# Causal attention in a two-layer block: the causal mask of the transposed scores moves from TensorE to a GpSimd select on the probabilities, and PV of two key tiles stand together

## The chip, the cores and the metric

One core of one Trainium2 chip. The metric is the device time of one execution in microseconds; the time of before is the median of its runs, 2668.89 us.

## The reference

Two layers on x of shape (2, 2048, 256), each with a layer norm, an attention s, a mixture of experts passed through silu, g, and x + s * g. The change touches the attention of the first layer alone. It is exact causal softmax attention of 16 heads of 16 columns:

```python
scores = jnp.einsum('bhcd,bhsd->bhcs', qi, k) * scale
mask = kpos[None, :] <= qpos[:, None]
scores = jnp.where(mask, scores, jnp.finfo(scores.dtype).min)
p = jax.nn.softmax(scores, axis=-1)
return (None, jnp.einsum('bhcs,bhsd->bhcd', p, v))
```

## The kernel before, in words

The program runs stage after stage: projections of the first layer, its attention (`stage_attention`), its experts, a join, and the second layer in windows. An engine's instructions run in the order in which its function lists them.

`stage_attention` works in 8 groups: 4 groups of 4 heads (GH) for each of the 2 sequences. A group has 4 chunks of 512 queries (QC, CH). Each chunk c looks at 4 (c + 1) key tiles of 128 keys, 40 in a group and 320 in all. The last 4 tiles of a chunk hold the diagonal; there only the queries from `lo` on are used, so that the widths are 512, 384, 256 and 128. Every attention has two passes:

- The maxima pass ("A"). Scores with queries on the partitions go to one of three PSUM banks, `ring` (L721, and L724 adds the mask `mask_qk` on the diagonal block). VectorE takes the maximum (L859, `take`). After each chunk VectorE splits the negated maxima into three bf16 parts (`split`, L866 to L870), TensorE turns them (L731), VectorE copies them out (L876), and SyncE's queue puts them into three more rows of `qa` (L691).
- The probabilities pass. "S" is the score with keys on the partitions (L774) for one head: the three more rows subtract the row's maximum. Two heads share a buffer `pss`, of which there are two. On a diagonal tile L777 adds `mask_kq`, -1e30 above the diagonal, by a second matmul against the identity on the first 128 columns. ScalarE takes the exponential of two heads in one instruction (L836) into `probs`, which keeps two key tiles: four slots of two heads. "PV" (L792) multiplies the probabilities with v, four heads side by side, each with 32 columns of the array, and gathers in `acc`; a column of ones in `vg` gathers the sum. It is fp32; each product has two records in the profile. At the end of a chunk ScalarE copies `acc` to `sums` ("COPY", L844); TensorE transposes that through the ring ("O", L802), VectorE divides (L906, L909), and ScalarE's queue stores it.

The order is written out by `attention_steps`. `weave` goes over the 40 pairs (chunk, key tile): it lists 4 S, puts as many steps of the maxima pass between them as their share of the columns asks for, and then lists the PV of the pair before. So PV of tile n - 1 stands behind the scores of tile n. The maxima run half a group ahead (LEAD): the second half of a group's own maxima, then the first half of the next group's; the last group has only its own second half. O and the turn of the maxima come 6 scores late. GpSimd has no part in this: in this stage it sets constants, clears the table of the experts and issues 32 scatters (L668). 

TensorE's waits: a score of the first head of two waits until the exponential that used the same `pss` is done; a maxima matmul waits until VectorE has taken the bank three steps back; PV waits for the second exponential of its tile. ScalarE's exponential waits for its scores and for the PV that used the same slots of `probs`.

Of the kernel before, what the change touches and what calls it, by code (L numbers as in the profile page):

```python
# [16 lines left out]
BF16 = mybir.dt.bfloat16  # L17
# [3 lines left out]
ALU = mybir.AluOpType  # L21
ACT = mybir.ActivationFunctionType
X = mybir.AxisListType.X

P = 128
B, S, D = 2, 2048, 256
T = B * S
NT = T // P
CH = 512
TC = CH // P  # L30
# [5 lines left out]
NEG = -1e30  # L36
# [7 lines left out]
GH = 4  # L44
HG = H // GH
KT = S // P
QC = S // CH
QR = 6 * HD
MR = QR + 3
# [56 lines left out]
def build_constants(nc, keep):  # L106

    with ExitStack() as ctx:
        st = Stage(nc, ctx, "c_")
# [4 lines left out]
        def _(pool):  # L114
            ch = Chain(pool, pool_step)
            ch.link(pool.memset(keep["identity"][:, :], 0.0))
            ch.link(pool.affine_select(out=keep["identity"][:, :], in_=keep["identity"][:, :], compare_op=ALU.not_equal,
                                       fill=1.0, base=0, pattern=[[-1, P]], channel_multiplier=1))
# [8 lines left out]
                                       fill=NEG, base=0, pattern=[[-1, P]], channel_multiplier=1))  # L127
            ch.link(pool.affine_select(out=keep["mask_kq"][:, :], in_=keep["zero16"][:, :], compare_op=ALU.is_ge,
                                       fill=NEG, base=0, pattern=[[1, P]], channel_multiplier=-1))

# [362 lines left out]
def attention_steps():  # L493
# [39 lines left out]
    def weave(ahead):  # L533
# [15 lines left out]
        for n, (c, j) in enumerate(pairs):  # L549
            for h in range(GH):  # L550
                steps.append(("S", c, j, h))
                done += width(c, j)
                advance()
                for item in late:
                    item[1] -= 1
                while late and late[0][1] <= 0:
                    steps.append(late.pop(0)[0])
            if n:
                pc, pj = pairs[n - 1]
                steps.append(("PV", pc, pj))  # L560
                if pj == TC * (pc + 1) - 1:
                    steps.append(("COPY", pc))
                    late.append([("O", pc), 6])
        c, j = pairs[-1]
        steps += ahead + [u for u, _ in late] + [("PV", c, j), ("COPY", c), ("O", c)]
        return steps
# [10 lines left out]


def stage_attention(nc, io, keep, dram):

# [4 lines left out]
    n_s = sum(u[0] == "S" for u in steps) // 2  # L585
    n_pv = sum(u[0] == "PV" for u in steps)
    parts_q, parts_k = (0, 0, 1, 1, 0, 2), (0, 1, 0, 1, 2, 0)
    n_loads = len(parts_q) * QC + len(parts_k)
    with ExitStack() as ctx:
# [3 lines left out]
        vg = [st.sb(f"vg{u}", [P, KT, GH, 32]) for u in range(2)]  # L593
        probs = st.sb("probs", [P, 4, 2, CH])
        best = st.sb("best", [P, QC, GH * TC, QC])
        neg = st.sb("neg", [P, GH * TC])
        neg_rest = st.sb("neg_rest", [P, GH * TC])
        neg_parts = st.sb("neg_parts", [P, P // (GH * TC), GH * TC], BF16)
        neg_rows = st.sb("neg_rows", [3 * GH * TC, 2, P], BF16)
        sums = st.sb("sums", [P, CH])  # L600
        inv = st.sb("inv", [P, TC, GH])
# [13 lines left out]
        m_landed = [st.sem(f"m_landed{c}") for c in range(QC)]  # L615
        o_stored = [st.sem(f"o_stored{c}") for c in range(2)]
        dve_step = st.sem("dve_step")
        cleared, scattered = st.sem("cleared"), st.sem("scattered")
# [33 lines left out]
        def _(pool):  # L652
# [14 lines left out]
            for t in range(NT):  # L667
                pool.indirect_dma_start(dram["expert_in"], bass.IndirectOffsetOnAxis(ap=keep["slot_put"][:, t:t + 1], axis=0),  # L668
                                        keep["xn_all"][:, t, :], None, bounds_check=E * CAP0 - 1, oob_is_err=False
                                        ).then_inc(scattered, 16)  # L670
            pool.wait_ge(scattered, 16 * NT)

# [41 lines left out]
        def _(pe):  # L714
# [34 lines left out]
            for g, i, u, order in groups(pe):  # L749
                idx = pv = m = r = 0  # L750
                next_seen = False
                for s in order:
# [11 lines left out]
                    elif s[0] == "S":  # L764
# [6 lines left out]
                        if e == 0:  # L771

                            pe.wait_ge(exp_done, primed + g * n_s + max(idx - 1, 0))
                        ins = pe.matmul(pss[idx % 2][:, e, lo:CH], kb[u][0:MR, h, j * P:(j + 1) * P],  # L774
                                        qa[u][0:MR, c, h, lo:CH], start=True, stop=(j < TC * c))
                        if j >= TC * c:
                            ins = pe.matmul(pss[idx % 2][:, e, lo:lo + P], keep["identity16"][:, :],  # L777
                                            keep["mask_kq"][:, :], start=False, stop=True)
                        if e == 1:
                            ins.then_inc(s_ready, 1)  # L780
                            idx += 1
                    elif s[0] == "PV":
                        _, c, j = s
                        lo = max(0, j - TC * c) * P
                        pe.wait_ge(exp_done, primed + g * n_s + 2 * pv + 2)
                        if c == 0 and j == 0:
# [4 lines left out]
                        for h in range(GH):  # L791
                            ins = pe.matmul(acc[32 * h:32 * h + 32, lo:CH], vg[u][:, j, h, :],  # L792
                                            probs[:, 2 * (pv % 2) + h // 2, h % 2, lo:CH],
                                            start=(j == 0), stop=(j == TC * (c + 1) - 1))
# [13 lines left out]
        def _(act):  # L808
# [11 lines left out]
            for g, i, u, order in groups(act):  # L820
                idx = r = pv = r_turn = 0
                turned_at = None
                for s in order:
# [6 lines left out]
                    if s[0] == "S" and s[3] % 2 == 1:  # L830
# [3 lines left out]

                        act.wait_ge(pv_done, primed + g * n_pv + max(idx // 2 - 1, 0))
                        act.activation(probs[:, idx % 4, :, lo:CH], pss[idx % 2][:, :, lo:CH], ACT.Exp).then_inc(exp_done, 1)  # L836
                        idx += 1
# [1075 lines left out]
def make_program(nc, io, out, upto=7):  # L1913
# [9 lines left out]
    with ExitStack() as ctx:  # L1923
# [7 lines left out]
            "mask_qk": st.sb("mask_qk", [P, P], BF16),  # L1931
            "mask_kq": st.sb("mask_kq", [P, P], BF16),
            "expert": st.sb("expert", [P, E, NT]),
# [70 lines left out]
```

## Time and profile before

| | us |
|---|---|
| median of 3 runs | 2668.89 |
| lowest of them | 2668.31 |
| span of the profiled execution | 2692.8 |
| the first attention's busy stretch in it, 214 to 1157 us | 943.0 |

The profiled execution has no time of its own beside its span; the span is 23.9 us (0.9%) above the median of the timed runs. In the timeline a row gives start, duration, engine, line, operation, output and inputs, how many like it were merged, and in brackets the idle time before it and what ended it. PE is TensorE, PEld its weight load, DVE VectorE, ACT ScalarE, POOL GpSimd.

### The profile page before, as it was taken

The page shows a single profiled execution, that of the slowest core. Times are in us where ns is not written, and L with a number is a line of the kernel's source. Part 1 is how long each engine was busy: PE and PEld are TensorE (multiplying, and loading weights), DVE is VectorE, ACT ScalarE, POOL GpSimd, SP SyncE. Part 2 cuts the span into 40 slices and gives each one's busy share as a digit, 9 for nine tenths or more (in the row PEclk, how much of TensorE's full clock was granted, in tenths as well). Part 3 has the DMA queues.
Part 4 walks back from the last instruction along what each step waited for, and adds up shares of the span by engine and source line. Part 5 has one row for each costly group of instructions (what it writes and reads, how often), then busy time and mean ns, then how long its engine had stood idle before and what let it go on. Part 6 is the DMA issues. An engine that isn't in the chain of part 4 may idle for free. (4 is left out here: it accounts for less than half of the span.)

```text
span 2692.8 us, 51134 instructions
## 1 busy us (share of the span) xinstructions
PE 2451.3 (91%) x16420; PEld 1589.0 (59%) x16420; DVE 1846.2 (69%) x3682; ACT 1406.8 (52%) x2776; POOL 815.1 (30%) x647
## 2 busy tenths in 40 slices
PE   5648999999999999969977599999999999999999
PEld 4512333333333333358866477777777777777777
DVE  7757877877787777424438476777667767766776
ACT  3404655656565566755634255555555555555554
POOL 1070000000000000014425355554455555444553
PEclk9858999999999999989988699999999999999999
DMA  4574041321404040033257000000000000000000
GB/s 135 191 170 65 5 62 26 41 52 16 61 6 62 6 60 5 7 127 133 102 177 241 18 13 12 11 13 13 13 13 13 9 11 13 13 13 13 13 9 9
DMA packets 189865, 132.85 MB, mean 49 GB/s; under 512 B 99857, under 2 KB 177687, under 8 KB 189712
## 3 DMA queue, kind: packets, MB, share of 16 engines
q1 hardware_dynamic: 160048, 100.06, 15.4%
q10 hardware_dynamic: 24160, 14.16, 2.2%
q0 software_dynamic: 5504, 16.69, 1.7%
q8 instruction: 83, 1.36, 0.2%
q14 instruction: 70, 0.57, 0.1%
HBM read 84.43 MB, written 46.14 MB: 48 GB/s over the span
## 5 line engine op out<-in xcount | busy, mean ns | idle before, releaser
L859 DVE TENSOR_REDUCE a_best<-a_ring 128x1 f32<-128x512 f32 (+3 forms) x1280 | 700.9, 604 | 214.0 <-PE a_ring L721 123.0
L836 ACT ACTIVATE a_probs<-a_pss 128x1024 f32<-128x1024 f32 (+3 forms) x640 | 554.0, 895 | 452.6 <-PE a_pss L777 228.7
L721 PE MATMUL a_ring<-a_kb,a_qa 96*128 96x512 bf16 (+3 forms) x1280 | 453.0, 365 | 67.2 <-DVE a_best L859 32.3
L774 PE MATMUL a_pss<-a_qa,a_kb 99*128 99x512 bf16 (+3 forms) x1280 | 433.9, 353 | 15.6 <-issue 7.2
L1771 ACT ACTIVATE w_probs<-w_pss,w_top 128x256 f32<-128x256 f32 x512 | 239.0, 476 | 379.7 <-DVE w_top L1859 365.0
L1606 POOL TENSOR_TENSOR w_probs<-w_probs,w_inv 128x512 f32<-128x512 f32 x256 | 301.0, 1176 | 395.7 <-DVE w_inv L1865 386.3
L962 POOL TENSOR_TENSOR e_w_r<-e_w,e_w_r 128x1024 fp32r<-128x1024 f32 x28 | 67.0, 2402 | 1032.7 <-ACT e_w_r L1035 1032.7
L1629 PE MATMUL w_psw<-wqkv,w_xr 128*128 128x512 f32 x1152 | 301.5, 398 | 11.6 <-POOL w_xr L1563 11.6
L774 PEld LDWEIGHTS a_pss<-a_qa,a_kb 99*128 99x128 bf16 x1280 | 123.5, 98 | 302.6 <-ACT a_probs L836 224.5
L792 PE MATMUL a_acc<-a_probs,a_vg 128*32 128x512 f32 (+3 forms) x2560 | 299.9, 541 | 0.1
L1669 PE MATMUL w_pss<-w_kd,w_qt 128*128 128x256 f32 x1536 | 278.4, 310 | 0.0
L1859 DVE TENSOR_REDUCE w_top<-w_pss 128x2 f32<-128x512 f32 x256 | 176.8, 691 | 141.5 <-PE w_pss L1669 140.7
L721 PEld LDWEIGHTS a_ring<-a_kb,a_qa 96*128 96x128 bf16 x1280 | 126.4, 99 | 223.9 <-DVE a_best L859 128.6
L1629 PEld LDWEIGHTS w_psw<-wqkv,w_xr 128*128 128x128 f32 x1152 | 205.6, 190 | 47.6 <-POOL w_xr L1563 12.1
L1669 PEld LDWEIGHTS w_pss<-w_kd,w_qt 128*128 128x128 f32 x1536 | 222.0, 195 | 4.1
L1629 PE MATMUL w_psw<-we,w_xr 128*128 128x512 f32 x768 | 204.2, 401 | 0.0
L1710 PE MATMUL w_pso<-w_pt,w_v 128*64 128x128 f32 x2048 | 168.3, 285 | 0.1
L1689 PE MATMUL w_pst<-identity,w_probs 128*128 128x128 f32 x1024 | 155.7, 275 | 0.0
L1629 PEld LDWEIGHTS w_psw<-we,w_xr 128*128 128x128 f32 x768 | 134.9, 188 | 22.9 <-issue 0.2
L1689 PEld LDWEIGHTS w_pst<-identity,w_probs 128*128 128x128 f32 x1024 | 123.6, 140 | 31.2 <-issue 5.7
L1882 DVE SCALAR_TENSOR_TENSOR w_y<-w_psw,coef,w_y 128x256 f32<-128x256 f32 x224 | 108.3, 484 | 42.4 <-PE w_psw L1629 23.2
L1710 PEld LDWEIGHTS w_pso<-w_pt,w_v 128*64 128x64 f32 x2048 | 106.5, 136 | 49.6 <-issue 49.1
(223 smaller groups left out, 3771.2 us busy)
## 6 DMA issues: line engine op xcount, KB each, us to landing
e_w<-in_w SPq DMA_DIRECT2D x16, 1024.0 KB, 7.9
qk_parts<-p_parts SPq DMA_DIRECT2D x32, 384.0 KB, 3.7
a_qa<-qk_parts SPq DMA_DIRECT2D x192, 64.0 KB, 2.5
a_kb<-qk_parts SPq DMA_DIRECT2D x42, 256.0 KB, 9.5
p_xin<-in_x SPq DMA_DIRECT2D x8, 512.0 KB, 5.4
v_rows<-p_vout SPq DMA_DIRECT2D x8, 512.0 KB, 5.1
a_vg<-v_rows SPq DMA_DIRECT2D x32, 128.0 KB, 9.1
expert_in<-zero POOLq DMA_DIRECT2D x16, 256.0 KB, 8.3
```

Source lines behind the costliest of these rows:

```text
L721: ins = pe.matmul(bank[:, 0:keys], qa[u][0:QR, i // TC, h, (i % TC) * P:(i % TC + 1) * P], kb[u][0:QR, h, k * CH:k * CH + keys], start=Tru ...
L774: ins = pe.matmul(pss[idx % 2][:, e, lo:CH], kb[u][0:MR, h, j * P:(j + 1) * P], qa[u][0:MR, c, h, lo:CH], start=True, stop=(j < TC * c))
L792: ins = pe.matmul(acc[32 * h:32 * h + 32, lo:CH], vg[u][:, j, h, :], probs[:, 2 * (pv % 2) + h // 2, h % 2, lo:CH], start=(j == 0), stop=( ...
L836: act.activation(probs[:, idx % 4, :, lo:CH], pss[idx % 2][:, :, lo:CH], ACT.Exp).then_inc(exp_done, 1)
L859: vec.tensor_reduce(best[:, i // TC, h * TC + i % TC, k:k + 1], bank[:, 0:keys], X, ALU.max).then_inc(ring_taken, 1)
L1606: pool.tensor_tensor(probs[:, p % 4, :, :], probs[:, p % 4, :, :], inv[:, :, p:p + 1].to_broadcast([P, 2, 2 * P]), ALU.mult).then_inc(p_re ...
L1629: ins = pe.matmul(psw[bank][:, :], xr[a][:, src, k, :], moving(b, k), start=(m == 0), stop=(m == len(pairs) - 1))
L1669: ins = pe.matmul(scores, qt[a][:, p, :], keys[b][:, p, :, :], start=False, stop=(a, b) == PARTS[-1])
L1689: ins = pe.transpose(pst[r % 2][:, 2 * e + role, :], probs[:, p % 4, e, role * P:(role + 1) * P], keep["identity"][:, :])
L1710: ins = pe.matmul(pso[e * DH:(e + 1) * DH, p % 4, :], v[(u + 1 + role) % 2][:, h * DH:(h + 1) * DH], pt[:, p % 2, 2 * e + role, :], start= ...
L1771: ins = act.activation(probs[:, p % 4, e, :], pss[p % 2][:, e, :], ACT.Exp, bias=top[:, e, p:p + 1], accum_out=rows[:, e, p:p + 1])
L1859: vec.tensor_reduce(top[:, :, p], pss[p % 2][:, :, :], X, ALU.max, negate=True).then_inc(top_ready, 1)
```

## The change

- The mask matmul on the transposed scores (L777) is gone, with its constant `mask_kq`. A score of a diagonal tile is written without a mask.
- After the exponential of a diagonal tile GpSimd sets the probabilities of future keys to zero in place, on 2 heads x 128 columns, by an `affine_select`; ahead of it stands an addition of one element per partition into a scratch tile `spare`. GpSimd does so behind its 32 scatters, for every diagonal exponential of all groups.
- PV of a diagonal tile waits for that (`future_cleared`), PV of another tile for the exponential as before.
- PV is listed for two tiles at a time: behind the scores of every even tile n stand PV of n - 2 and of n - 1; the last two of a group stand at its end.
- `probs` keeps four key tiles (KEPT), so that ScalarE waits for the PV four tiles back instead of two.

```diff
-            if n:
-                pc, pj = pairs[n - 1]
+            for pc, pj in (pairs[n - 2], pairs[n - 1]) if n and n % 2 == 0 else ():
                 steps.append(("PV", pc, pj))
                 if pj == TC * (pc + 1) - 1:
                     steps.append(("COPY", pc))
                     late.append([("O", pc), 6])
-        c, j = pairs[-1]
-        steps += ahead + [u for u, _ in late] + [("PV", c, j), ("COPY", c), ("O", c)]
+        c = pairs[-1][0]
+        steps += ahead + [u for u, _ in late] + [("PV", *p) for p in pairs[-2:]] + [("COPY", c), ("O", c)]
...
+KEPT = 4
...
+    n_diagonal = QC * TC * GH // 2
...
-        probs = st.sb("probs", [P, 4, 2, CH])
+        probs = st.sb("probs", [P, KEPT * GH // 2, 2, CH])
...
+            for g, i, u, order in groups(pool):
+                idx = 0
+                for s in order:
+                    if s[0] == "S" and s[3] % 2 == 1:
+                        _, c, j, h = s
+                        if j >= TC * c:
+                            lo, slot = (j - TC * c) * P, idx % (KEPT * GH // 2)
+                            pool.wait_ge(exp_done, primed + g * n_s + idx + 1)
+                            pool.tensor_tensor(spare[:, slot:slot + 1], keep["zero"][:, 0:1], keep["zero"][:, 0:1], ALU.add)
+                            seen = probs[:, slot, :, lo:lo + P]
+                            pool.affine_select(out=seen, in_=seen, compare_op=ALU.is_ge, fill=0.0, base=0,
+                                               pattern=[[0, 2], [1, P]], channel_multiplier=-1).then_inc(future_cleared, 1)
+                        idx += 1
             pool.wait_ge(scattered, 16 * NT)
...
                         ins = pe.matmul(pss[idx % 2][:, e, lo:CH], kb[u][0:MR, h, j * P:(j + 1) * P],
-                                        qa[u][0:MR, c, h, lo:CH], start=True, stop=(j < TC * c))
-                        if j >= TC * c:
-                            ins = pe.matmul(pss[idx % 2][:, e, lo:lo + P], keep["identity16"][:, :],
-                                            keep["mask_kq"][:, :], start=False, stop=True)
+                                        qa[u][0:MR, c, h, lo:CH], start=True, stop=True)
...
-                        pe.wait_ge(exp_done, primed + g * n_s + 2 * pv + 2)
+                        if j < TC * c:
+                            pe.wait_ge(exp_done, primed + g * n_s + 2 * pv + 2)
+                        else:
+                            pe.wait_ge(future_cleared, g * n_diagonal + GH // 2 * (j + 1))
...
-                                            probs[:, 2 * (pv % 2) + h // 2, h % 2, lo:CH],
+                                            probs[:, GH // 2 * (pv % KEPT) + h // 2, h % 2, lo:CH],
...
-                        act.wait_ge(pv_done, primed + g * n_pv + max(idx // 2 - 1, 0))
-                        act.activation(probs[:, idx % 4, :, lo:CH], pss[idx % 2][:, :, lo:CH], ACT.Exp).then_inc(exp_done, 1)
+                        act.wait_ge(pv_done, primed + g * n_pv + max(idx // 2 - KEPT + 1, 0))
+                        act.activation(probs[:, idx % (KEPT * GH // 2), :, lo:CH], pss[idx % 2][:, :, lo:CH], ACT.Exp).then_inc(exp_done, 1)
```

## Rows read from the trace of the kernel before

**Rows 1.** The head of the page: span, busy time by engine.

```profile
span 2692.8 us, 51134 instructions
...
PE 2451.3 (91%) x16420; PEld 1589.0 (59%) x16420; DVE 1846.2 (69%) x3682; ACT 1406.8 (52%) x2776; POOL 815.1 (30%) x647
```

**Rows 2.** Busy time by engine in windows: us, PE, PEld, DVE, ACT, POOL, clock, DMA.

```profile
214.00:1157.00 943.00, 899.55 (x6196) 339.54 (x6196) 711.99 (x1459) 569.05 (x672) 0.00 (x0) 0.99 0.22 33
```

**Rows 3.** Groups of instructions by line, 214 to 1157 us.

```profile
L859 DVE TENSOR_REDUCE a_best<-a_ring 128x1 f32<-128x512 f32 (+3 forms) x1215 | 667.8, 606 | 173.5 <-PE a_ring L721 119.4 <-PE a_ring L724 47.1 <-remote 4.5
L836 ACT ACTIVATE a_probs<-a_pss 128x1024 f32<-128x1024 f32 (+3 forms) x640 | 554.0, 895 | 452.6 <-PE a_pss L777 228.7 <-PE a_pss L774 207.8 <-DVE a_best L859 10.1
...
L792 PE MATMUL a_acc<-a_probs,a_vg 128*32 128x512 f32 (+3 forms) x2560 | 299.9, 541 | 0.1
...
L777 PE MATMUL a_pss<-mask_kq,identity 128*128 128x128 bf16 x512 | 104.9, 222 | 0.0
```

**Rows 4.** Timeline of TensorE around a first diagonal tile.

```profile
1048.67 0.39 PE L774 MATMUL a_pss<-a_qa,a_kb 99*128 99x512 bf16 x1
1048.89 0.22 PE L777 MATMUL a_pss<-mask_kq,identity 128*128 128x128 bf16 x1
1048.95 0.38 PE L721 MATMUL a_ring<-a_kb,a_qa 96*128 96x512 bf16 x1
...
1050.73 0.22 PE L724 MATMUL a_ring<-mask_qk,identity 128*128 128x128 bf16 x1
1050.88 1.06 PE L792 MATMUL a_acc<-a_probs,a_vg 128*32 128x512 f32 x8
1051.88 0.34 PE L774 MATMUL a_pss<-a_qa,a_kb 99*128 99x384 bf16 x1
```

**Rows 5.** Window over eight key tiles without a diagonal.

```profile
656.46:683.09 26.63, 25.80 (x157) 8.67 (x156) 21.80 (x47) 15.96 (x17) 0.00 (x0) 1.00 0.03 7
```

**Rows 6.** Timeline in the same stretch: VectorE, and TensorE's PV and next maxima matmul.

```profile
665.28 2.35 DVE L859 TENSOR_REDUCE a_best<-a_ring 128x1 f32<-128x512 f32 x4 [0.84 <-PE a_ring L721]
...
666.54 1.06 PE L792 MATMUL a_acc<-a_probs,a_vg 128*32 128x512 f32 x8
...
667.77 0.38 PE L721 MATMUL a_ring<-a_kb,a_qa 96*128 96x512 bf16 x1
...
668.19 2.88 DVE L859 TENSOR_REDUCE a_best<-a_ring 128x1 f32<-128x512 f32 x6 [0.56 <-PE a_ring L721]
...
671.70 1.29 DVE L859 TENSOR_REDUCE a_best<-a_ring 128x1 f32<-128x512 f32 x2 [0.63 <-PE a_ring L721]
```

**Rows 7.** Who waited for whom in the same stretch: in all, times, longest.

```profile
PEld a_ring L721 <- DVE a_best L859: 3.5, 10, 0.5
```

**Rows 8.** Timeline at the end of a group.

```profile
1057.38 1.01 PE L792 MATMUL a_acc<-a_probs,a_vg 128*32 128x256 f32 x16
1057.96 0.16 PEld L792 LDWEIGHTS a_acc<-a_probs,a_vg 128*32 128x32 f32 x8 [0.43 <-ACT a_probs L836]
...
1059.10 0.66 PE L802 MATMUL a_ring<-identity,a_sums 128*128 128x128 f32 x4 [0.70 <-ACT a_sums L844]
```

**Rows 9.** Timeline of the tail, where no maxima are left.

```profile
1133.42 3.91 ACT L836 ACTIVATE a_probs<-a_pss 128x1024 f32<-128x1024 f32 x4 [0.27 <-PE a_pss L774]
...
1133.75 1.07 PE L792 MATMUL a_acc<-a_probs,a_vg 128*32 128x512 f32 x8
...
1137.59 3.90 ACT L836 ACTIVATE a_probs<-a_pss 128x1024 f32<-128x1024 f32 x4 [0.26 <-PE a_pss L774]
```

**Rows 10.** Timeline of GpSimd in three places: start, last scatter, masks of layer two.

```profile
0.44 0.10 POOL L1999 MEMSET const-float32-0.0<- 128x1 f32 x1 [0.44 <-issue]
...
209.42 0.98 POOL L668 DMA_INDIRECT expert_in<-xn_all,slot_put  x1 [0.30 <-issue]
...
1513.55 0.29 POOL L1587 TENSOR_SCALAR_AFFINE_SELECT w_before_mask<-w_before_mask 128x128 bf16<-128x128 bf16 x1
...
1515.85 2.00 POOL L1587 TENSOR_SCALAR_AFFINE_SELECT w_even_masks<-w_even_masks 128x2048 bf16<-128x2048 bf16 x1
```

More of the change, by code:

```diff
@@ L127, in _ @@
                                        fill=NEG, base=0, pattern=[[-1, P]], channel_multiplier=1))
-            ch.link(pool.affine_select(out=keep["mask_kq"][:, :], in_=keep["zero16"][:, :], compare_op=ALU.is_ge,
-                                       fill=NEG, base=0, pattern=[[1, P]], channel_multiplier=-1))
             ch.link(pool.iota(keep["expert"][:, :, :], pattern=[[1, E], [0, NT]], base=0, channel_multiplier=0,
@@ L599, in stage_attention @@
         neg_rows = st.sb("neg_rows", [3 * GH * TC, 2, P], BF16)
+        spare = st.sb("spare", [P, KEPT * GH // 2])
         sums = st.sb("sums", [P, CH])
@@ L616, in stage_attention @@
         o_stored = [st.sem(f"o_stored{c}") for c in range(2)]
+        future_cleared = st.sem("future_cleared")
         dve_step = st.sem("dve_step")
@@ L1931, in make_program @@
             "mask_qk": st.sb("mask_qk", [P, P], BF16),
-            "mask_kq": st.sb("mask_kq", [P, P], BF16),
             "expert": st.sb("expert", [P, E, NT]),
```

## The prediction

> **What bounds the kernel now.** I read the page's head first: TensorE is busy for 91% of the 2692.8 us span and no other engine is near it [rows 1]. The change touches one stage, so next come the windows. The first attention stage runs from 214 to 1157 us, 943 us; in it TensorE is busy for 899.55 us, VectorE for 712, ScalarE for 569 and GpSimd for nothing [rows 2]. The groups of that stage say what the busy time is: 512 mask matmuls on L777, 2560 records of PV on L792 (each fp32 product has two records, a key tile has 8), 640 exponentials and 1215 maxima [rows 3].
>
> Busy time is not a price: a record also covers the pipeline. The price is the distance from start to start. A 512-column score takes 0.22 us, a mask 0.06 us (1048.89 to 1048.95), and a PV of one key tile starts 0.15 us after the start of a 0.06 us mask and holds the next score back by 1.00 us (1050.88 to 1051.88) [rows 4]. Of this 1.10 us, 0.853 is work (4 passes of 512 columns at 2.4 GHz; the granted clock is 0.99 there [rows 2]). So about 0.24 us go in and out of each PV.
>
> Does TensorE wait although it looks full? In a stretch of eight key tiles without a diagonal, 26.63 us, TensorE shows 25.80 busy, and VectorE 21.80: 3.33 us a tile, of which VectorE works 2.73 and idles 0.60 [rows 5]. The timeline tells when: PV starts at 666.54, VectorE empties the ring at 665.28 + 2.35 = 667.63, then has nothing until 668.19, since the next maximum's matmul starts only at 667.77, behind PV and one score [rows 6]. The next idle spots, 0.56 and 0.63 us, look alike. In the same stretch TensorE's loads waited 10 times for VectorE, 3.5 us in all [rows 7]. So PV starves VectorE, and VectorE, through a ring of three banks, then holds TensorE. A tile without waits would take 3.05 us (four scores 0.88; PV 1.10; of the stretch's 157 records [rows 5] 64 are PV and 32 scores, most of the other 61 are some 37 maxima matmuls and their masks, 1.07 us a tile); the other 0.28 are waits. TensorE alone is not the bound here; the pair is.
>
> **The masks.** The 512 matmuls on the diagonal tiles go: 512 x 0.058 = 30 us of TensorE time at most. In the diagonal tiles a score is narrower, so fewer maxima lie between and VectorE has slack: most of it is real there. But the first diagonal tile of a chunk is full width, and the last chunk of the program has ScalarE as its bound (below).
>
> **Pairing PV.** Before, 312 of the 320 tiles switch in and out on their own; at each group's end two already stand side by side. After, there are 160 pairs: 152 switches fewer. A switch is worth 0.24 less what a join costs. The one join in the trace starts its second half 0.58 us after the first, where 256 columns are 0.43 us of work, but it waited for ScalarE [rows 8]; so the join costs between nothing and 0.15, and I take 0.05: 0.19 x 152 = 29 us at most.
>
> The Trainium skill, TensorEngine Tiling (Array Packing), section Key Properties, says that a change of the tiling mode drains TensorE. The 0.24 us agrees; by that rule alone pairing would bring 0.24 x 152 = 36 us. It says nothing of who starves meanwhile.
>
> Now the price of pairing. The ring keeps three banks. Today the next maximum is ready 1.65 us after a PV starts (668.19 - 666.54) and VectorE has 1.09 us of work left at that start [rows 6]. A second PV behind the first adds 0.853 + 0.05, so 2.55 us. VectorE has 1.09 to 1.3 us left (never more than three reductions, 1.62 at 0.54 each: 12 of them in 6.52 us), and idles 1.25 to 1.46 us per pair where it now idles 2 x 0.60. Two tiles then take 2 x 2.73 + 1.25 to 1.46 = 6.7 to 6.9 us, against 6.66: I take +0.15. The ends are 2 x 2.73 + 2.55 - 1.62 = 6.39 (-0.27), with a full ring before each PV pair, and 7.0 (+0.35), where ScalarE's chain interferes too. There are 12 such pairs in a group, 96, 90 without the tail: +13 us, between -24 and +31.
>
> ScalarE's chain: only two score buffers exist, whatever the number of kept probabilities. In the tail after 1122 us, without maxima, two tiles take 4.17 us (1137.59 - 1133.42), four exponentials of 1.02 with 0.26 idle [rows 9]. With PV in pairs the cycle is: last exponential done, two scores 0.44, 0.10 into PV, PV pair 1.95, two scores 0.44, 0.2 to the start of ScalarE, two exponentials 2.04: 5.2 us. So +1.0 for each of 6 pairs: +6 us (3 to 8). With maxima between, the same loop is 6.1 us, just under VectorE's 6.8. The four kept tiles of probabilities cost nothing in themselves; without them ScalarE would wait for the PV pair too.
>
> **The select.** Each of the 512 / 2 = 256 diagonal exponentials (one for two heads) gets a one-element add and a select of 2 x 128 fp32 on GpSimd, in place, before PV may read. A select took 0.29 us for 128 columns and 2.00 for 2048, so 0.41 for 256; a one-element operation took 0.10 [rows 10]. With the hops, 0.65 us from the exponential to the release; I allow 0.5 to 1.5. GpSimd is idle otherwise: its last scatter issue ends at 210.4 [rows 10], ahead of the first PV. In the middle of a group the select is mostly covered: TensorE has two more scores and the maxima between (0.9 us) after the exponential it waited for, and GpSimd's backlog of the narrow last tile clears while a full-width tile is scored. But in the first diagonal pair (384 and 256 columns) ScalarE and then GpSimd are the chain: exponentials 0.8 + 0.8, select 0.65, so some tenths are lost where the masks gave. At a group's end nothing covers it: now the last PV waits 0.43 us in the weight load for ScalarE, and then the transposes of the sums [rows 8]; after, it waits for two selects in a row behind two 0.33 us exponentials, 1.0 us later. Behind that PV are the copy, the transposes and the next group: 8 x 1.0 = +8 us (4 to 12). This is the wait that the change adds.
>
> Diagonal chunks: masks 16 x 0.058 = 0.93, two switches 0.38, together 1.3 us at most. VectorE needs its idle time in each PV pair here too, and ScalarE with the select takes some. I take half, 0.7, in 31 chunks: -22 us (0 to -40).
>
> The Trainium skill's GPSIMD Engine Reference, Specifications, says that GpSimd's SBUF interfaces are shared with VectorE where a VectorE instruction has two SBUF inputs. The maxima have one, from PSUM. Two short subtractions per chunk do have two; if GpSimd is selecting for 5 of 29 us and each such meeting costs a select, that is about 64 x 0.17 x 0.41 = 4 us, an estimate that no row here bears out.
>
> **Sum.** -22 + 13 + 6 + 8 = +5 us. The profiled execution spans 2692.8 us, 24 more than the 2668.89 us median; a difference of this size is not changed by the ratio 0.991. Forecast: 2674 us, no difference that a measurement tells (about 2%, or 53 us, is what it can tell from no change). The ends of the terms add up to -57 (-40, -24, +3, +4) and +51 (0, +31, +8, +12).
>
> **Rivals.**
> First: TensorE is the bound after all and every removed microsecond counts. For it: 95% busy in the stage, and only 3.5 us of waits in 26.63. Against it: VectorE's idle spot after every PV. Then -30 - 29 + 8 + 5 (short waits for the select) = -46: 2623 us; with the full 0.24 a switch and masks off a waiting chain as well, 2611. Chance 0.24, half of it beyond 2%.
> Second, slower: the select is the chain. Place: the PV pair on the diagonal waits for GpSimd, and everything behind it on TensorE, scores and maxima of the next pass, stands. It decides once one exponential's select takes over 1 us with its hops. At 1.5 us, 64 pairs lose 0.85 and 8 group ends 2: +70, masks and switches -22, the rest +7: 2724 us. Against it: 0.41 us by the two select rows. Chance 0.14.
> Third: pairing starves both readers of PSUM at the upper end: 90 x 0.35 = +31, tail +8, group ends +8, diagonals -10: +37, 2706 us. Chance 0.12.
> The change not doing what it says: with the select at zero instead of the mask the sums are the same, only PV moves; a wrong clock gate is not likely at 0.99 now.
> The forecast keeps 0.50.
>
> **Numbers.** Range 2620 to 2724, up to both far rivals. Likeliest case alone: 2650 to 2700. Faster by over 2%: half of the first rival and a little, 0.14. Slower by over 2%: the second rival and the edge of the third, 0.17. Within 2%: 0.69.
>
> **What would show it.** L777 gone; PV in groups of 16 records, about 1.9 us from start to the next score; VectorE idle 1.3 to 1.5 us once per pair of full tiles and VectorE's idle time over the stage not smaller; two tiles near 6.8 us; the tail's cycle at 5.2 us instead of 4.17; a last PV at each group's end that waits for GpSimd, about 1 us; a select near 0.41 us. I am wrong if two full tiles take 6.3 us or less (the ring did not hold), or if TensorE waits for GpSimd in the middle of groups for more than 0.3 us a time.

## The result and the profile after

The changed kernel takes 2701.18 us (median of 4 runs) against 2668.60 us for the kernel before in the same session: 32.6 us more by the medians, and a ratio of 1.0132 with a 95% interval of 1.0112 to 1.0153, which is 35 us. That is slower, clearly so, and within 2%. One of the four executions of before took 9096.91 us; the ratio leaves it out.

The head of the page of after:

```profile
span 2700.3 us, 50915 instructions
...
PE 2430.2 (90%) x15908; PEld 1574.2 (58%) x15908; DVE 1838.8 (68%) x3682; ACT 1409.7 (52%) x2776; POOL 953.3 (35%) x1158
```

Beside [rows 1]: 512 TensorE instructions fewer and 21 us less busy time, yet the kernel is slower. The span grew by 7.5 us only, since the profiled execution of before was a long one: 24 us over its own median. Below it turns out where these 24 us were.

The groups by line of after, 197 to 1168 us, for comparison with [rows 3] (whose window, 214 to 1157 us, begins behind the stage's first waits):

```profile
L875 DVE TENSOR_REDUCE a_best<-a_ring 128x1 f32<-128x512 f32 (+3 forms) x1199 | 649.8, 605 | 200.5 <-PE a_ring L737 100.7 <-PE a_ring L740 98.5
L852 ACT ACTIVATE a_probs<-a_pss 128x1024 f32<-128x1024 f32 (+3 forms) x640 | 552.4, 895 | 442.9 <-PE a_pss L790 426.4 <-DVE a_best L875 7.5
L790 PE MATMUL a_pss<-a_qa,a_kb 99*128 99x512 bf16 (+3 forms) x1280 | 432.3, 357 | 37.7 <-ACT a_probs L852 19.0 <-issue 8.0 <-DMA a_qa<-a_neg_rows 7.1
L737 PE MATMUL a_ring<-a_kb,a_qa 96*128 96x512 bf16 (+3 forms) x1198 | 422.9, 359 | 32.3 <-DVE a_best L875 28.0
L808 PE MATMUL a_acc<-a_probs,a_vg 128*32 128x512 f32 (+3 forms) x2560 | 271.8, 541 | 17.1 <-POOL a_probs L684 17.1
...
L684 POOL TENSOR_SCALAR_AFFINE_SELECT a_probs<-a_probs 128x256 f32<-128x256 f32 x256 | 104.2, 407 | 0.0
...
L682 POOL TENSOR_TENSOR a_spare<-zero 128x1 f32<-128x1 f32 x256 | 49.5, 193 | 814.9 <-ACT a_probs L852 813.3
```

The mask group is gone. PV is busy for 272 us instead of 300, as its switches are halved. But the idle time in front of the maxima rose from 173.5 to 200.5 us (12.4 us of it in a single wait at the start, which comes below), scores now wait for ScalarE (19.0 us, where the waits view of before has 2.4), and PV waits for GpSimd (17.1 us, 9.1 of them in one wait at the start). A select takes 0.407 us; the one-element add ahead of it 0.193 us.

Two full tiles with their pair, the timeline where [rows 6] showed single PVs:

```profile
655.97 1.92 PE L808 MATMUL a_acc<-a_probs,a_vg 128*32 128x512 f32 x16
...
658.53 4.67 DVE L875 TENSOR_REDUCE a_best<-a_ring 128x1 f32<-128x512 f32 x9 [1.37 <-PE a_ring L740]
...
662.03 1.92 PE L808 MATMUL a_acc<-a_probs,a_vg 128*32 128x512 f32 x16
...
664.54 4.08 DVE L875 TENSOR_REDUCE a_best<-a_ring 128x1 f32<-128x512 f32 x8 [1.33 <-PE a_ring L737]
```

VectorE is idle for 1.37 and 1.33 us behind every pair, and its first maximum starts 2.56 us after the pair's start (2.55 was forecast). The tail, for [rows 9]:

```profile
1139.26 3.77 ACT L852 ACTIVATE a_probs<-a_pss 128x1024 f32<-128x1024 f32 x4 [1.26 <-PE a_pss L790]
...
1141.79 1.92 PE L808 MATMUL a_acc<-a_probs,a_vg 128*32 128x512 f32 x16
...
1143.65 1.04 PE L790 MATMUL a_pss<-a_qa,a_kb 99*128 99x512 bf16 x4
1144.29 3.77 ACT L852 ACTIVATE a_probs<-a_pss 128x1024 f32<-128x1024 f32 x4 [1.25 <-PE a_pss L790]
```

Two tiles take 5.03 us there (1144.29 - 1139.26) instead of 4.17; ScalarE idles 1.26 instead of 0.26. The pair itself takes 1.86 us from its start to the next score; one PV takes 1.00, of which 0.853 is work. So the second PV adds 0.86 us, just its work: the join costs nothing that can be measured.

**Where in the stage.** The copy of the sums at the end of each chunk is a good clock. Before, from one group, and after, from the same group:

```profile
500.32 0.59 ACT L844 COPY a_sums<-a_acc 128x512 f32<-128x512 f32 x1
...
536.10 0.58 ACT L844 COPY a_sums<-a_acc 128x512 f32<-128x512 f32 x1
...
581.49 0.58 ACT L844 COPY a_sums<-a_acc 128x512 f32<-128x512 f32 x1 [0.55 <-PE a_acc L792]
...
595.28 0.58 ACT L844 COPY a_sums<-a_acc 128x512 f32<-128x512 f32 x1 [0.34 <-PE a_acc L792]
```

```profile
490.87 0.59 ACT L860 COPY a_sums<-a_acc 128x512 f32<-128x512 f32 x1
...
528.18 0.59 ACT L860 COPY a_sums<-a_acc 128x512 f32<-128x512 f32 x1
...
574.19 0.59 ACT L860 COPY a_sums<-a_acc 128x512 f32<-128x512 f32 x1 [1.41 <-PE a_acc L808]
...
588.53 0.59 ACT L860 COPY a_sums<-a_acc 128x512 f32<-128x512 f32 x1 [1.45 <-PE a_acc L808]
```

The third chunk took 35.78 us and takes 37.31, the fourth 45.39 and 46.01. These intervals repeat from group to group, mostly to 0.1 us, with two exceptions. The second chunk of a group is some us longer where a DMA is late (below). And the change from the second group to the third and from the fourth to the fifth takes about 5 us more than the others. The program's loop over the groups has two groups in its body and turns there, and TensorE stands still without a wait that the profile shows. Timeline of before, then the windows view from that place (us, PE, PEld, DVE, ACT, POOL, clock, DMA):

```profile
463.58 0.60 PE L774 MATMUL a_pss<-a_qa,a_kb 99*128 99x512 bf16 x1 [3.65 <-issue]
```

```profile
463.50:470.00 6.50, 6.42 (x24) 3.16 (x25) 3.85 (x7) 2.86 (x3) 0.00 (x0) 0.50 0.52 114
```

Every profile here has both of these pauses, of 3.5 to 4.1 us; behind this one the granted clock is 0.50 for 6.5 us. They explain no difference between the kernels. The table has, for each kernel, the shortest of each interval over the first six groups and the five changes between them: second, third, fourth chunk, and the next group's first; then the tail's chunk, and the time from the first copy to the last.

| kernel | chunk 2 | chunk 3 | chunk 4 | next 1 | sum | tail | first to last |
|---|---|---|---|---|---|---|---|
| before | 21.97 | 35.77 | 45.39 | 13.79 | 116.9 | 30.31 | 917.5 |
| after | 21.51 | 37.30 | 46.01 | 14.07 | 118.9 | 36.50 | 943.4 |
| e1 select alone | 21.15 | 35.47 | 45.55 | 13.53 | 115.7 | 30.91 | 920.6 |
| e2 pairs alone | 21.91 | 37.46 | 45.54 | 14.26 | 119.2 | 36.09 | 936.2 |
| e5 select, v late | 21.15 | 35.47 | 45.53 | 13.53 | 115.7 | 30.90 | 903.8 |
| e6 before, v late | 21.97 | 35.75 | 45.38 | 13.79 | 116.9 | 30.31 | 909.9 |
| e7 no mask, no select | 21.10 | 35.22 | 44.68 | 13.31 | 114.3 | 29.73 | 916.4 |
| e8 select, lag of two | 20.56 | 34.84 | 42.70 | 15.88 | 114.0 | 28.85 | 886.2 |
| e9 before, half maxima | 20.99 | 33.63 | 42.66 | 13.33 | 110.6 | 30.31 | 882.0 |
| e10 pairs, half maxima | 21.10 | 34.54 | 42.83 | 13.47 | 111.9 | 36.09 | 893.0 |
| e11 masks, lag of two | 21.43 | 35.14 | 42.96 | 16.11 | 115.6 | 29.07 | 899.6 |
| e12 after, both waits mended | 21.51 | 37.31 | 46.02 | 14.06 | 118.9 | 36.50 | 934.4 |

From first copy to last, after loses 25.9 us. Another 10 us are lost before the first copy, which after has at 221.77 us and e2, the same without the select, at 211.50. (The profile of before has it at 237.25, since that execution was a long one.)

### The profile page after: what moved, and what is told of

Same layout as the page of the kernel before. It is cut to its first block and busy times, and to the rows that moved or that the text cites. A ratio compares the mean times of both kernels' runs of the same rounds, so it can differ in the third digit from the quotient of the medians.

```text
span 2700.3 us, 50915 instructions
## 1 busy us (share of the span) xinstructions
PE 2430.2 (90%) x15908; PEld 1574.2 (58%) x15908; DVE 1838.8 (68%) x3682; ACT 1409.7 (52%) x2776; POOL 953.3 (35%) x1158
## 3 DMA queue, kind: packets, MB, share of 16 engines
q1 hardware_dynamic: 160048, 100.06, 15.2%
## 5 line engine op out<-in xcount | busy, mean ns | idle before, releaser
L875 DVE TENSOR_REDUCE a_best<-a_ring 128x1 f32<-128x512 f32 (+3 forms) x1280 | 690.3, 603 | 220.2 <-PE a_ring L740 117.8
L737 PE MATMUL a_ring<-a_kb,a_qa 96*128 96x512 bf16 (+3 forms) x1280 | 460.8, 370 | 58.9 <-DVE a_best L875 29.5
L682 POOL TENSOR_TENSOR a_spare<-zero 128x1 f32<-128x1 f32 x256 | 49.5, 193 | 814.9 <-ACT a_probs L852 813.3
L808 PE MATMUL a_acc<-a_probs,a_vg 128*32 128x512 f32 (+3 forms) x2560 | 271.8, 541 | 17.1 <-POOL a_probs L684 17.1
L790 PEld LDWEIGHTS a_pss<-a_qa,a_kb 99*128 99x128 bf16 x1280 | 119.2, 99 | 253.2 <-issue 118.1
L808 PEld LDWEIGHTS a_acc<-a_probs,a_vg 128*32 128x32 f32 x2560 | 66.7, 110 | 148.7 <-issue 113.3
```

The lines of the kernel that those rows point to most:

```text
L737: ins = pe.matmul(bank[:, 0:keys], qa[u][0:QR, i // TC, h, (i % TC) * P:(i % TC + 1) * P], kb[u][0:QR, h, k * CH:k * CH + keys], start=Tru ...
L875: vec.tensor_reduce(best[:, i // TC, h * TC + i % TC, k:k + 1], bank[:, 0:keys], X, ALU.max).then_inc(ring_taken, 1)
```

## The experiments

**e1 and e2: each half of the change alone.** e1 keeps the select and puts PV back to one tile at a time:

```diff
-            for pc, pj in (pairs[n - 2], pairs[n - 1]) if n and n % 2 == 0 else ():
+            for pc, pj in (pairs[n - 1],) if n else ():
...
-        steps += ahead + [u for u, _ in late] + [("PV", *p) for p in pairs[-2:]] + [("COPY", c), ("O", c)]
+        steps += ahead + [u for u, _ in late] + [("PV", *p) for p in pairs[-1:]] + [("COPY", c), ("O", c)]
...
-KEPT = 4
+KEPT = 2
```

> The select on GpSimd instead of the mask matmuls, PV of one tile at a time, two key tiles kept as before. Theory P (the pairing of PV is what costs: it starves VectorE and ScalarE): the masks give back some 20 us, the first PV waits about 12 us for GpSimd to be done with its scatters, group ends lose about 1 us each; together about 2665 to 2672 us, no slower than before. Theory S (the select's waits are what costs): about 2695 us, nearly as slow as after, with many waits of PV on GpSimd of over 0.3 us in the middle of groups.

e2 is the kernel before with the new list of PVs and KEPT = 4, mask matmuls kept, nothing on GpSimd:

```diff
-            if n:
-                pc, pj = pairs[n - 1]
+            for pc, pj in (pairs[n - 2], pairs[n - 1]) if n and n % 2 == 0 else ():
...
-        probs = st.sb("probs", [P, 4, 2, CH])
+        probs = st.sb("probs", [P, KEPT * GH // 2, 2, CH])
```

> The mask matmuls stay on TensorE, no select; PV in pairs, four key tiles kept. Theory P: slower than before by 20 to 35 us, 2690 to 2702 us, the tail's cycle of two tiles at 5.0 us. Theory S: faster than before by the transitions saved, 2645 to 2660 us.

Measured: e1 1.0045 (1.0028 to 1.0061) of before, 2682.82 us against 2672.06, some 12 us slower by the ratio. e2 1.0082 (1.0060 to 1.0103), 2690.94 us, some 22 us slower. By the ratios the two add up to 34 us, and the whole change is 35. The pairing is the larger loss, as theory P has it, at the low end of its range; but e1 came out between the theories, 10 us over P's figure. So the select costs too, and the table says it is mostly not in the body of the chunks: a group of e1 is 1.2 us shorter than before, 10 us over 8 groups, and still first to last is 3 us longer.

**What e1 lost.** Part one is the start. Timeline of after (e1's is alike, with a wait of 9.62 us):

```profile
203.66 0.38 PE L737 MATMUL a_ring<-a_kb,a_qa 96*128 96x512 bf16 x1
...
210.85 0.98 POOL L671 DMA_INDIRECT expert_in<-xn_all,slot_put  x1 [0.30 <-issue]
211.89 0.19 POOL L682 TENSOR_TENSOR a_spare<-zero 128x1 f32<-128x1 f32 x1
212.04 0.40 POOL L684 TENSOR_SCALAR_AFFINE_SELECT a_probs<-a_probs 128x256 f32<-128x256 f32 x1
...
213.18 1.08 PE L808 MATMUL a_acc<-a_probs,a_vg 128*32 128x512 f32 x4 [9.14 <-POOL a_probs L684]
```

The first PV stands ready at 204 and waits until GpSimd has issued its last scatter and reached the selects. Behind PV stand all scores and maxima. After the wait the granted clock is 0.50 in the 4 us from 213, and the first pair takes 3.2 us instead of 1.92. Windows view of after:

```profile
213.00:217.00 4.00, 3.82 (x20) 1.01 (x21) 0.00 (x0) 0.24 (x1) 2.01 (x8) 0.50 0.34 32
```

Part two is a wait in the other queue. The waits on the maxima's rows, before, then e1 (the waits view, 225 to 1175 us):

```profile
PE a_pss L774 <- DMA a_qa<-a_neg_rows: 5.8, 4, 1.6
...
PEld a_pss L774 <- DMA a_qa<-a_neg_rows: 1.9, 1, 1.9
```

```profile
PE a_pss L790 <- DMA a_qa<-a_neg_rows: 12.7, 4, 3.7
...
PEld a_pss L790 <- DMA a_qa<-a_neg_rows: 3.5, 1, 3.5
```

and the timeline of e1 around one of them:

```profile
580.55 14.58 SPq L699 DMA_DIRECT2D a_vg<-v_rows  x3
...
595.26 3.06 SPq L707 DMA_DIRECT2D a_qa<-a_neg_rows  x3
...
599.60 0.39 PE L790 MATMUL a_pss<-a_qa,a_kb 99*128 99x512 bf16 x1 [3.65 <-DMA a_qa<-a_neg_rows]
```

SyncE's queue is held by the loads of the next group's v until 595.1; only then does it issue the row store on which the first score of a chunk waits. Counted from the group's start this moment does not move when TensorE gets faster, and the wait takes the gain: 16.2 us where before had 7.7. The waits differ from execution to execution (3.5 us in e2, 7.1 in after, 15.2 in e3).

**e3: the scatters early.**

```diff
             ch = Chain(pool, set_up)
...
-            table = dram["expert_in"].rearrange("(p a) d -> p (a d)", p=P)
-            n = table.shape[1] // CH
-            for k in range(n):
-                pool.dma_start(table[:, k * CH:(k + 1) * CH], keep["zero"][:, :]).then_inc(cleared, 16)
```

(the four lines move ahead of `ch = Chain(pool, set_up)`, before the memsets.)

> The changed kernel, with the clearing of the experts' table issued ahead of GpSimd's memsets, so that the 32 scatters are issued earlier and GpSimd is free when the first diagonal exponential is done. If TensorE's 9.1 us wait at the first PV is paid in full: about 12 us less than after, 2689 us (with the clock's drop behind it). If it is hidden by something later: 2700 us.

Measured: 1.0093 (1.0077 to 1.0110), 2697.65 us. Against 1.0132 for after, that is 0.4% or 10 us less, though the two ratios are of two sessions and the difference is uncertain by some 7 us. In the profile PV's wait is 0.24 us instead of 9.14, and the first copy comes at 212.63 instead of 221.77; in e2 it is at 211.50. So up to the first copy the wait was paid in full. The span of this profile is only 3.0 us shorter, since its scores waited 15.2 us for the maxima's rows where after's waited 7.1.

**e4: the last group unpaired.**

```diff
+            if paired:
+                ripe = pairs[n - 2:n] if n and n % 2 == 0 else []
+            else:
+                ripe = pairs[n - 1:n] if n else []
+            for pc, pj in ripe:
...
-    return head, weave(stream), weave(flow(lead, len(maxima), 0))
+    return head, weave(stream), weave(flow(lead, len(maxima), 0), False)
```

> The changed kernel, with PV of one tile at a time in the last group alone, where the second half has no maxima. By the tail's cycles (5.03 us against 4.17 for two tiles, and the last chunk's 36.5 us against 30.3): 5 to 8 us less than after, about 2695 us. If the select in that chunk is what takes the time: no change or more.

Measured: 1.0076 (1.0059 to 1.0092), 2693.14 us. In the profile the tail's chunk takes 30.91 us instead of 36.50; the ratios of after and e4 lie 0.56% apart, 15 us, more than the profile has, but they come from two sessions and their intervals all but meet. ScalarE's blocks of four exponentials start 4.17 us apart again, with the select in place: the tail is lost to the pairing and not to the select.

**e5 to e8** ran on one chip, where before takes 2697.38 us; each ratio is to that.

e5 is e1 with e3's edit, and with the loads of v behind the first row store:

```diff
-                load_v(first, u)
...
+                values_due = not (isinstance(g, int) and g == 2 * HG - 1)
                 for r, s in enumerate(s for s in order if s[0] in in_ring):
                     if s[0] == "MT":
                         store_rows((u + s[1]) % 2, s[2], r_head + g * n_ring + r)
+                        if values_due:
+                            load_v(first, 1 - u)
+                            values_due = False
```

> The select with PV of one tile at a time, scatters issued early, and in SyncE's queue the loads of the next group's v behind the first store of the maxima's rows instead of ahead of it. If e1's loss was the wait for the scatters at the start (some 11 us) and the score that waits for the row DMA (16 us over the run against 8 before), and the masks' time in the middle is real (10 us by the chunk intervals): 2650 to 2660 us, faster than before by 0.5% or so. If the middle of the groups is what e1 lost: 2670 us or more.

e6 has that last edit on the kernel before, and nothing else.

> The kernel before with only the loads of v moved behind the first store of the rows. The waits on the row DMA were 7.7 us in all there: 2661 to 2665 us if that is all; no change if the row's DMA is late for another reason.

Measured: e5 0.9942 (0.9928 to 0.9955), 15 us faster than before; e6 0.9979 (0.9970 to 0.9988), 6 us faster. The absolute 2650 to 2660 us that e5's text names is of the other chip; the share, 0.5%, came out. In both profiles no score waits for the rows any more. So the wait for the rows was part of what e1 lost, and with it gone the masks' time shows: e5 is 10 us under e6, as a group is 1.2 us shorter. The early scatters of e5 are not tested here. On this chip even e7, with late scatters, has its last scatter done at 211.9 us and its first PV at 231.7, so there was no wait at the start to be mended; that part rests on e3.

e7 is e1 without GpSimd's loop, PV waiting for ScalarE alone; it leaves the mask of the probabilities out, so that its result is wrong.

```diff
-                        if j < TC * c:
-                            pe.wait_ge(exp_done, primed + g * n_s + 2 * pv + 2)
-                        else:
-                            pe.wait_ge(future_cleared, g * n_diagonal + GH // 2 * (j + 1))
+                        pe.wait_ge(exp_done, primed + g * n_s + 2 * pv + 2)
```

> As the select alone (PV of one tile at a time, late scatters), but with the causal mask of the probabilities left out altogether: no mask matmul and no select, PV waits for ScalarE alone. It prices the masks without the select. By my prediction's term (16 masks of 0.058 us in a chunk, half of it lost) the chunk intervals fall by about 0.5 us against before; if VectorE is the bound there, they fall by less than 0.2. Against the select alone, the group ends are 1.0 us shorter each and the start 11 us: about 2655 to 2662 us.

Measured: 0.9983 (0.9974 to 0.9993). As a total it is a miss, since its waits on the row DMA are 13.6 us; the intervals are what it was made for. A group falls by 2.6 us, 0.65 per chunk: of the 0.93 us of a chunk's 16 mask matmuls two thirds are won. The select gives 1.4 us of these 2.6 back (e1's group is 115.7 us, e7's 114.3), most of it, 0.87 us, at the end of the fourth chunk.

e8 is e5 with PV of one tile, two tiles behind the scores:

```diff
-            for pc, pj in (pairs[n - 1],) if n else ():
+            for pc, pj in (pairs[n - 2],) if n > 1 else ():
...
-KEPT = 2
+KEPT = 4
```

> As e5_select_late_values, with PV of one tile at a time but two tiles behind the scores instead of one (four key tiles kept). If the select's waits in the middle of groups cost something, it is 2 to 6 us faster than e5; if only the group ends wait, it is equal or some us slower, since two PVs are left for the end of each group.

Measured: 0.9890 (0.9875 to 0.9905), 2665.95 us: 30 us faster than before and 0.5% faster than e5, more than expected. It is the fastest version here that keeps both passes whole. (e5 and e6 are faster than before too.)

**e9 to e12**, again on one chip (before: 2698.93 us). e9 and e10 halve what VectorE has to read; they compute the maxima over the first half of their columns only. (A row's maximum is only a shift of the exponent and cancels in the division.)

```diff
-                vec.tensor_reduce(best[:, i // TC, h * TC + i % TC, k:k + 1], bank[:, 0:keys], X, ALU.max
+                vec.tensor_reduce(best[:, i // TC, h * TC + i % TC, k:k + 1], bank[:, 0:keys // 2], X, ALU.max
```

> The kernel before, with each maximum taken over the first half of its columns only, so that VectorE needs about 0.27 us less for each of 1280; all else as before. It shows how much of the stage is VectorE's: if the pair of TensorE and VectorE is the bound, as I read it, 25 to 50 us faster than before; if TensorE alone is, under 10.

> PV in pairs with the mask matmuls kept (e2), with the same halved maxima. Against e9 on the same chip: if VectorE's empty ring is what made the pairs slower, the pairs now gain in the body and lose only the tail's 6 us: 5 to 20 us faster than e9. If ScalarE's two score buffers are the cause, the pairs stay slower than e9 by 15 to 30 us.

Measured: e9 0.9833 (0.9800 to 0.9866), e10 0.9856 (0.9831 to 0.9881). Groups by line of e9, 240 to 1150 us:

```profile
L859 DVE TENSOR_REDUCE a_best<-a_ring 128x1 f32<-128x256 f32 (+3 forms) x1166 | 431.7, 384 | 332.5 <-PE a_ring L721 214.7 <-PE a_ring L724 97.6
```

A maximum takes 384 ns in the mean instead of 606 [rows 3]. With TensorE's work untouched the kernel is 45 us faster by the ratio: VectorE's time bounds the stage together with TensorE's. And with VectorE light the pairs cost 10 us in the medians and 11 us from first copy to last, of which the tail is 5.8; in the body 5 us are left of the 13 that the table shows for e2 (936.2 - 917.5, less 5.8). The ratios of e9 and e10 overlap in their intervals, so this rests on the profiles. By the intervals a group of pairs was 2.3 us longer, and now it is 1.3. So a maximum shorter by a third takes away between two and three fifths of the body's loss: that part is VectorE's. Neither expectation is met, for the pairs still don't gain in the body. What the rest of the body's loss is stays open. ScalarE's two buffers are a candidate (TensorE's scores wait 14.5 us for ScalarE in e10 and 3.8 in e9, tail included), but no run gives ScalarE a third one. The tail has no maxima; there ScalarE's cycle is the bound, 36.09 us in e2 and e10 alike.

e11 asks whether e8 needs the select: mask matmuls kept, lag of two, v late.

> The kernel before (mask matmuls on TensorE, no select) with PV of one tile at a time two tiles behind the scores, four key tiles kept, and the loads of v behind the first row store. If the gain of e8 (1.1% under before) is the lag's and the select brings nothing: 1% under before or more. If the select's saved TensorE time is what counts and the lag only hides the select: 0.2 to 0.4% under before, as e6.

Measured: 0.9929 (0.9905 to 0.9953), 19 us faster than before by the ratio (17 by the medians), where e6, the same without the lag, is 6 us faster. So e8's 30 us are about: 6 for the late v (e6), 13 for the lag (e11 over e6), and 11 for the masks off TensorE (e8 over e11). The last two compare ratios of two chips and are uncertain by some 7 us each; from first copy to last the profiles give 10.3 for the lag and 13.4 for the masks. Neither expectation alone was right: the lag helps with the masks too.

e12 is the changed kernel with both outer waits mended.

> The changed kernel with the scatters early and the loads of v behind the first row store. What is left against e5 (the same with PV of one tile at a time) is the pairing alone: 18 to 24 us over e5, that is about 0.3 to 0.4% over before. If pairing with the select costs less than with the masks: equal to before or under it.

Measured: 1.0041 (1.0029 to 1.0054), against e5's 0.9942: the pairing costs 1.0%, 27 us, beside the select, where e2 has 22 beside the masks. By the ratios alone the two can't be told apart, but the intervals say the same: a group of pairs is 3.2 us longer beside the select (e12 and e5) and 2.3 beside the masks (e2 and before). So beside the pairs the masks' removal brings next to nothing: a group of e12 is 0.3 us shorter than one of e2, where single PVs gave 1.2. Why is not shown.

## Why the prediction was right, and where not

The forecast was 2674 us, no difference that can be told, range 2620 to 2724. The time, 2701 us, lies in the range and within 2% of before, but it is 33 us over before and not 5, and the difference is clear of noise. The range held because it was wide, up to two far rivals, and not because the sum did. Sorted anew, with the chunks' intervals and the first copies:

| | forecast | measured |
|---|---|---|
| pairing: full tiles, tail, switches of diagonal chunks | +13 | +23 (17 body, 6 tail) |
| masks off TensorE, with the select's waits | -8 | -2 |
| SyncE's queue: late rows | none | +5 (11 in after, 6 in before) |
| the wait for the scatters at the start | none | +10 |

The forecast's -22 for diagonal chunks is divided as its 0.93 us of masks and 0.38 of switches. The pairing is e2 against before, 18.7 us from first copy to last, and 4 more because its rows were less late; late rows are what the second chunks take over the shortest. The measured terms come to 36 us, and the ratio says 35. By the steps:

- *TensorE and VectorE bound the body together.* Right. Shown by e9: 45 us with a maximum shorter by a third. The first rival (TensorE alone, 2623 us) falls, with e2 as well.
- *The masks are worth 0.7 us a chunk, with the switches, in all -22.* Beside single PVs the masks alone gave 0.65 a chunk (e7), -21 in all, and with the select -10 (e1's groups). Beside the pairs, for which the term was written, masks and select together gave about -2 (e12 against e2, 0.3 us a group). That PV in pairs would take the gain was not seen.
- *Pairing, full tiles: +13 (-24 to +31).* The mechanism was right: 2.56 us to the first maximum and 1.33 to 1.37 us of idle time. The base of the sum was off: I took 6.66 us for two tiles from a stretch of eight that held a transposition of the sums. From the PV of the second full tile to that of the twelfth, that chunk had 6.41 us for two tiles (660.32 to 692.36), and after has 6.30 (pairs at 655.97 and 687.49). So the sign of error that the prediction names, 6.3 us or less, was reached there, just, in the fourth chunk. In the third chunk two tiles went from 6.20 (624.63 to 643.22) to 6.57 us (618.66 to 638.37), and that is where e2 loses 1.7 of its 2.3 us a group. A gain in the one and a loss in the other: without the tail the pairing cost 13 (copies) to 16 us (ratio), or 17 with fewer late rows counted out. That is near the term and inside its bounds, by a sum whose parts did not hold one by one, and this part is luck.
- *The tail, +6.* 5.8 (e2), the cycle 5.03 for a forecast 5.2.
- *The select at the group's end, +8.* Right in place and size: 0.87 us a group between e7 and e1, 7 us in all. Timeline of after at the end of a group, for [rows 8]:

```profile
572.05 0.64 PE L808 MATMUL a_acc<-a_probs,a_vg 128*32 128x256 f32 x8
572.12 0.66 ACT L852 ACTIVATE a_probs<-a_pss 128x256 f32<-128x256 f32 x2 [1.61 <-PE a_pss L790]
...
573.24 0.41 POOL L684 TENSOR_SCALAR_AFFINE_SELECT a_probs<-a_probs 128x256 f32<-128x256 f32 x1
...
573.70 0.43 PE L808 MATMUL a_acc<-a_probs,a_vg 128*32 128x128 f32 x8 [1.01 <-POOL a_probs L684]
```

  The last PV waits 1.01 us for the second of two selects.
- *GpSimd "is idle otherwise: its last scatter issue ends at 210.4, ahead of the first PV".* This step failed, for 10 to 11 us (e3, and the first copies of e1 and e2). In the profile of before the first PV is at 229.6 us, so it looked safe by 19 us. That execution was 24 us over the median, and they were lost just there: from 186 to 214 us VectorE stood still several times (below). In the profiles of after and e2, which are near their medians, the first PV is ready at 204. The note that span and median differ by 24 us stood in the prediction; where these 24 us lie was not asked.
- *SyncE's queue* was in no term. The row store behind the loads of v caps the gain at a group's start. The waits themselves are 7.1 us in after and 7.7 in before, but three second chunks of after are 3.1 to 4.7 us longer than its shortest (26.19, 24.62 and 24.87 against 21.51). With the queue mended, e12 takes 934.4 us from first copy to last instead of 943.4, and e6 takes 909.9 instead of 917.5.
- *Two subtractions a chunk that meet the select, some 4 us.* None of them met one (last section); what met it was a cast, for 3 us.

The second rival's mechanism (the select as a chain in the middle of groups) is real only to 1.4 us a group, not 70 us. Inside the groups of after the waits of PV's loads for GpSimd are 0.2 to 0.4 us each (one of 0.7 right behind the start), so the sign of error set at 0.3 us was barely touched.

## What to carry to other kernels

Two matmul groups side by side save a mode switch (0.24 us here), but they also silence the engines that live from the other matmuls: count how long the ring of PSUM banks lasts against the longer gap before grouping. Delaying PV by one more tile, one at a time, had the same four kept tiles and gained some 13 us where pairing lost 22. And when the profiled span stands far from the median, find the stretch in which it does before reading any slack from that place.

## What the hardware showed unexpectedly

Between 183 and 214 us, while GpSimd issued scatters, the profile of before shows maxima that wait up to 4.91 us for a releaser that the profile calls remote:

```profile
193.20 0.69 DVE L859 TENSOR_REDUCE a_best<-a_ring 128x1 f32<-128x512 f32 x1 [4.91 <-remote]
195.99 0.69 DVE L859 TENSOR_REDUCE a_best<-a_ring 128x1 f32<-128x512 f32 x1 [2.10 <-remote]
...
203.69 0.29 DVE L859 TENSOR_REDUCE a_best<-a_ring 128x1 f32<-128x128 f32 x1 [4.90 <-remote]
```

The profiles of after and e2 have back-to-back maxima there instead. In the sessions of e5 to e12 every profile has a late start (first copy at 231 to 243 us), and before takes 2697 to 2699 us instead of 2669 to 2672. With so late a start the first PV comes after the last scatter even where the scatters are late, so the wait of e1 and after belongs to the quick executions alone. The cause stays open; no run here was made for it.

A select lengthens a VectorE instruction that it meets, though not one of those that I had weighed. Groups by line, before (300 to 1400 us), then after (197 to 1168 us):

```profile
L867 DVE CAST a_neg_parts<-a_neg 128x16 bf16<-128x16 f32 x27 | 4.7, 174 | 0.9
```

```profile
L883 DVE CAST a_neg_parts<-a_neg 128x16 bf16<-128x16 f32 x30 | 8.0, 265 | 1.0
```

The mean hides two kinds. Timeline of after, in two places:

```profile
524.82 0.41 POOL L684 TENSOR_SCALAR_AFFINE_SELECT a_probs<-a_probs 128x256 f32<-128x256 f32 x1
524.84 0.42 DVE L883 CAST a_neg_parts<-a_neg 128x16 bf16<-128x16 f32 x1
525.28 0.17 DVE L884 TENSOR_TENSOR a_neg_rest<-a_neg,a_neg_parts 128x16 f32<-128x16 f32 x1
...
546.38 0.17 DVE L883 CAST a_neg_parts<-a_neg 128x16 bf16<-128x16 f32 x1
```

Of the 30 first casts of a split 15 overlap a select; they take 0.29 to 0.42 us and end within 0.04 us of the select's end. The other 15 overlap none and take 0.17 us. e1 divides in the same way, and in e2, without a select, every such cast behind the scatters takes 0.17 or 0.18 us. In all that is 3 us. The reduction just ahead of the cast (L882) overlaps selects too and keeps its 0.18 to 0.20 us. The Trainium skill, GPSIMD Engine Reference, Specifications, names two kinds of VectorE instructions that contend with GpSimd for SBUF, those with two SBUF inputs and those in a two-port mode. No run here shows the first kind, since the subtractions of after never overlap a select; in which mode the cast ran no row says.

A join of two PVs cost nothing measurable: 1.86 us for a pair, 1.00 for one, 0.853 being the work. By the Trainium skill, TensorEngine Tiling (Array Packing), Key Properties, only a change of the mode drains the array; the trace agrees. And a 9 us wait of TensorE was followed by a stretch at a granted clock of 0.50, 1.2 GHz.
